# Attention's value product in two passes per head, with high and low values side by side in the stationary operand, and some weight sums moved behind attention

## The reference

```python
def _L0_xattn_ref(q, latent_kv, Wq, Wkv_expand, Wout):
    ...
    k, v = jnp.split(kv, 2, axis=-1)
    ...
    scores = jnp.einsum('bhqd,bhkd->bhqk', qh, kh) * inv_sqrt_d
    scores = jnp.where(causal, scores, jnp.finfo(scores.dtype).min)
    attn = jax.nn.softmax(scores, axis=-1)
    out = jnp.einsum('bhqk,bhkd->bhqd', attn, vh)
    return out.transpose(0, 2, 1, 3).reshape(b, sq, H) @ Wout.T

def weight_quant(w):
    scale = 1.0 / jnp.clip(jnp.mean(jnp.abs(w)), EPS_Q, None)
    return jnp.clip(jnp.round(w * scale), -1, 1) / scale

x = x + _L0_xattn_ref(_layernorm(x), ctx_512, Wq, Wkv_expand, Wout)
x = x + _L0_attn_ref(_layernorm(x), w_gate, norm_gate, w_down, norm_down)
x = x + _L0_ffn_ref(_layernorm(x), rms_weight, router_w, w_gate, w_up, w_down, sw_gate, sw_up, sw_down)
```

## Time and profile before

| | us |
|---|---|
| median of 3 runs | 635.94 (635.56 to 636.33) |
| span of the profiled execution | 633.0 |
| median less span | 2.9 |
| TensorE matmul busy in the span | 611.9 (97%) |
| VectorE busy | 524.0 (83%) |
| ScalarE busy | 421.6 (67%) |
| GpSimd busy | 148.1 (23%) |
| mean granted TensorE clock | 0.998 of full speed |

### The profile page before, as it was taken

How to read it: one execution, slowest core, us unless ns; L and a number is a source line. 1 busy time by engine, 2 the same in 40 slices (tenths; PEclk the granted TensorE clock), 3 DMA queues, 4 the chain that set the end, 5 groups by cost and what they waited for, 6 DMA issues and landing times.

```text
span 633.0 us, 10577 instructions
## 1 busy us (share of the span) xinstructions
PE 611.9 (97%) x3624; PEld 475.4 (75%) x3625; DVE 524.0 (83%) x886; ACT 421.6 (67%) x558; POOL 148.1 (23%) x167
## 2 busy tenths in 40 slices
PE   8899999998999999999989999999999999999996
PEld 6678888887886444444557888898988989889775
DVE  5888888878787777889999479789797988979686
ACT  4998888889755989784574366639376483855630
POOL 2354446416000333527920310000000000000051
PEclk9999999999999999999999999999999999999999
DMA  8977776765246997936999558796775968759257
GB/s 337 420 291 298 301 303 238 310 267 191 100 174 260 403 362 286 400 134 241 402 364 416 216 204 325 262 370 224 299 315 200 390 210 319 273 219 393 86 176 264
DMA packets 31070, 177.91 MB, mean 281 GB/s; under 512 B 4064, under 2 KB 4064, under 8 KB 14784
## 3 DMA queue, kind: packets, MB, share of 16 engines
q1 hardware_dynamic: 25536, 158.64, 65.3%
q0 software_dynamic: 5504, 18.88, 8.2%
HBM read 154.30 MB, written 23.20 MB: 280 GB/s over the span
## 4 chain that ended last, share of the span: by engine, by line
PE 50%; DVE 19%; ACT 14%; issue 8%; DMA 5%; POOL 2%; DVEq 1%; POOLq 0%; ACTq 0%; SPq 0%
PE BK L2132 10%; PE BK L306 9%; DVE WL L1029 4%; ACT RA L1383 4%; ACT PR L1410 4%; PE BK L2135 3%; PE BK L1882 3%; PE BK L312 3%; PE BK L318 3%; PE BK L313 3%; DMA RA<-wbit 2%; PE BK L2102 2%; PE BK L1827 2%; DMA RX<-wbit 1%; PE BK L2155 1%
## 5 line engine op out<-in xcount | busy, mean ns | idle before, releaser
L2132 PE MATMUL BK<-EX,WH 128*128 128x320 f32 x384 | 101.3, 344 | 0.3
L1029 DVE TENSOR_TENSOR WL<-RA,WH 128x2048 fp32r<-128x2048 f32 x40 | 89.4, 2287 | 7.6 <-ACT WH L1586 7.4
L2135 PE MATMUL BK<-EX,WL 128*128 128x160 f32 x336 | 79.3, 236 | 0.0
L1586 ACT ACTIVATE WH<-RA 128x2048 fp32r<-128x2048 f32 x40 | 73.6, 1910 | 0.2 <-PE BK L1925 0.2
L2132 PEld LDWEIGHTS BK<-EX,WH 128*128 128x128 f32 x384 | 69.7, 188 | 1.9 <-DVE SR L1069 1.9
L2135 PEld LDWEIGHTS BK<-EX,WL 128*128 128x128 f32 x336 | 64.1, 191 | 0.0
L705 POOL DMA_INDIRECT GA<-rows,SLOT x4 | 4.9, 1229 | 240.4 <-DVE WL L1029 239.5
L652 POOL TENSOR_TENSOR HB<-HB,ND (+2 forms) x26 | 28.6, 1121 | 100.5 <-DVE BH L915 99.9
L1482 ACT ACTIVATE RA<-RA,RT 128x2048 int16<-128x2048 f32 x22 | 43.7, 1998 | 3.8 <-DMA RA<-wbit 1.9
L1029 DVE TENSOR_TENSOR WL<-RC,WH 128x2048 fp32r<-128x2048 f32 x20 | 45.0, 2285 | 0.7 <-ACT WH L1586 0.7
L1882 PE MATMUL BK<-TG,XQ 128*128 128x512 bf16 x192 | 42.4, 379 | 0.1
(11 more groups left out here) (328 smaller groups left out, 1644.1 us busy)
## 6 DMA issues: line engine op xcount, KB each, us to landing
RA<-wbit SPq DMA_DIRECT2D x54, 1024.0 KB, 6.7
RA<-wmoe SPq DMA_DIRECT2D x40, 1024.0 KB, 6.5
RC<-wmoe SPq DMA_DIRECT2D x20, 1024.0 KB, 8.0
rows<-ZERO POOLq DMA_DIRECT2D x40, 256.0 KB, 8.2
XG<-rows SPq DMA_DIRECT2D x10, 512.0 KB, 3.7
rows<-YS SPq DMA_DIRECT2D x9, 512.0 KB, 6.0
RA<-wqk SPq DMA_DIRECT2D x7, 640.0 KB, 7.8
RA<-wo SPq DMA_DIRECT2D x4, 1024.0 KB, 7.5
```

The source lines that it names most:

```text
L1029: e.tensor_tensor(WL[m][:, q * RAW:q * RAW + RAW], RC[j][:, :], WH[m][:, q * RAW:q * RAW + RAW].bitcast(f32), ALU.subtract)\
L1586: e.activation(WH[m][:, q * RAW:q * RAW + RAW], RC[2 * m + q][:, :], ACT.Copy)\
L2132: mm = e.matmul(bank[GBK[f]][:, 0:2 * R], WH[m][:, at], EX[:, k, :, :].rearrange("p a b -> p (a b)"), start=k == 0, stop=k == KD - 1)
L2135: e.matmul(bank[GBK[f]][:, 0:R], WL[m][:, at], EX[:, k, 0, :], start=False, stop=False)
```

## The change

- **Value product.** VS holds, for each of four key blocks, high values of head 0, low values of head 0, low values of head 1, high values of head 1, 64 columns each; there are no zeros. A head's stationary operand is its high and low values side by side. Its moving operand is PTH, then PTL: two passes of four matmuls a head, 16 in place of 24 a pair. Low values x low probabilities are now included. Head 0 accumulates in bank 2, head 1 in bank 7. Since bank 2 is part of head 0's score strip, head 0 starts only when `probs_lo` has read the strip, and the third mask of the next scores waits until bank 2 is evacuated.
- **Evacuation.** VectorE copies the products with high values to AO (`values_out`), ScalarE those with low values to BT (`low_values`), 64 partitions each, per head. GpSimd adds them and splits the sum into OTH and OTL (`out_split`, three operations a pair, one or two steps later). The last pair is added and split by VectorE and ScalarE.
- **Weight sums.** Four of the down chunks (29 to 32) are no longer summed in attention. RA[4] is not loaded in the steps any more, which now all have three sums. In ScalarE's step the sum of RA[3] comes right behind the exponentials and that of RA[1] before the query split; VectorE's sum of RA[2] comes before `probs_lo`. SP's order is RA[0], 1, 2, 3 as before. The four chunks are loaded into XQ's and RD's space and summed by ScalarE under the output projection (`late_load`, `late_absum`); the scale of the down weights is made later, by a matmul and `down_scales`.
- **Order.** In ScalarE's last step `wo_hi(0)` comes before the query split and `wo_hi(1)` behind `values_hi`. `k_split` of VectorE comes between the two halves of `probs_lo`. `down_load(1)` is issued later.

```diff
-        VH = a("VH", [P, NT, 3, HD], f32r)
-        VL = a("VL", [P, NT, 3, HD], f32r)
+        VS = a("VS", [P, NT, 4, HD], f32r)
+        BT = a("BT", [P, TOK], f32)
...
             for j in (1, 2, 3):
-                sum_load(j, 11 + j, 1)
-            sum_load(4, 10, 1)
+                sum_load(j, 9 + j, 1)
             e.dma_start(WR[:, :, :], wrt).then_inc(s("norm_in"), 16)
 
             def pair_loads(c):
                 qk_load(c)
                 for j in (1, 2, 3):
-                    sum_load(j, c * 3 + 8 + j, c)
-            for c in (2, 3, 4):
-                pair_loads(c)
-                sum_load(4, (11, 31, 32)[c - 2], c)
-            with e.Fori(5, NPAIR - 1) as c:
+                    sum_load(j, c * 3 + 6 + j, c)
+            with e.Fori(2, NPAIR - 1) as c:
                 pair_loads(c)
             qk_load(NPAIR - 1)
-            e.wait_ge(free_a[4], 5)
+            e.wait_ge(free_a[4], 1)
             wo_load(0)
-            sum_load(1, 30, NPAIR - 1)
+            sum_load(1, 28, NPAIR - 1)
             e.wait_ge(free_a[3], NPAIR - 1)
...
-            e.wait_ge(s("ot_lo"), NPAIR + 1)
+            e.wait_ge(s("av_pe"), 2 * NPAIR)
             e.dma_start(NG[:, :], n_gate.partition_broadcast(P)).then_inc(s("norm_in"), 16)
+
+            def late_load(j, chunk):
+                e.dma_start(DS[j][:, :], wbit[chunk]).then_inc(s(("raw_8", "raw_d")[j]), 16)
+            e.wait_ge(s("t_pe"), 2 * NPAIR)
+            late_load(0, 29)
 
             def bit_load(j, chunk, name, uses):
                 e.wait_ge(s(name), uses)
@@ -479,8 +486,13 @@
             def down_load(i, name):
                 e.dma_start(down_raw(i)[:, :], wbit[2 * GC + i]).then_inc(s(name) if isinstance(name, str) else name, 16)
             e.wait_ge(s("wo_d"), 2)
+            late_load(1, 30)
             for n in range(4):
                 bit_load(n, 4 + n, "tern", 1 + n)
+                if n in (1, 3):
+                    e.wait_ge(sum_x[0], 3 + n // 2)
+                    late_load(1, 31 + n // 2)
+            e.wait_ge(sum_x[0], 5)
             down_load(1, "raw_d")
...
+            def out_split(c):
+                at = bass.ds(c, 1)
+                e.wait_ge(s("av_ev1"), c * 2 + 4)
+                e.tensor_tensor(AO[:, :], AO[:, :], BT[:, :], ALU.add).then_inc(s("ot_hi"), 1)
+                e.wait_ge(s("ot_hi"), c * 2 + 1)
+                hi = OTH[:, at, :].rearrange("p a n -> p (a n)")
+                e.tensor_tensor(hi.rearrange("p (a b) -> p a b", b=P), AO[:, :].rearrange("p (a b) -> p a b", b=P),
+                                ONEF[:, :].rearrange("p (a b) -> p a b", a=1).to_broadcast([P, TOK // P, P]), ALU.mult)\
+                    .then_inc(s("ot_hi"), 1)
+                e.wait_ge(s("ot_hi"), c * 2 + 2)
+                e.tensor_tensor(OTL[:, at, :].rearrange("p a n -> p (a n)"), AO[:, :], hi.bitcast(f32), ALU.subtract)\
+                    .then_inc(s("ot_lo"), 1)
...
-            def probs_lo(c):
+            def probs_lo(c, between=None):
                 for h in range(2):
+                    if h and between is not None:
+                        k_split(between)
                     e.wait_ge(s("pt_hi"), c * 2 + h + 1)
                     e.tensor_tensor(PTL[h][:, :], STR[h][:, 0:STRIP], PTH[h][:, :].bitcast(f32), ALU.subtract)\
                         .then_inc(s("pt_lo"), 1)
 
-            def out_lo(c):
-                at = bass.ds(c, 1)
-                e.wait_ge(s("ot_hi"), c + 1)
-                e.tensor_tensor(OTL[:, at, :].rearrange("p a n -> p (a n)"), bank[7],
-                                OTH[:, at, :].rearrange("p a n -> p (a n)").bitcast(f32), ALU.subtract)\
-                    .then_inc(s("ot_lo"), 1)
+            def values_out(c, to=AO):
+                e.wait_ge(s("ot_lo"), c + 1 if to is AO else NPAIR - 1)
+                for h in range(2):
+                    e.wait_ge(s("av_pe"), c * 2 + h + 1)
+                    e.tensor_copy(to[HEADS[h], :], bank[VALUE_BANKS[h]][HEADS[h], :]).then_inc(s(("av_ev0", "av_ev1")[h]), 1)
...
             def pair(c, more):
                 row_maxima(c - 1)
                 normalise(c - 1)
-                k_split(c)
-                probs_lo(c - 1)
+                if more:
+                    absum(2, bass.ds(c * 3 + 8, 1), c * 16 + 16)
+                probs_lo(c - 1, c)
                 q_split(c)
-                if more:
-                    absum(2, bass.ds(c * 3 + 10, 1), c * 16 + 16)
-                else:
+                values_out(c - 1)
+                if not more:
                     wo_lo(0)
-                out_lo(c - 1)
...
+            values_out(NPAIR - 1, AO_LAST)
             wo_lo(2)
-            out_lo(NPAIR - 1)
+            e.wait_ge(s("av_ev0"), 2 * NPAIR)
+            e.wait_ge(s("av_ev1"), 2 * NPAIR + 2)
+            e.tensor_tensor(AO_LAST[:, :], AO_LAST[:, :], BO_LAST[:, :], ALU.add).then_inc(s("av_ev0"), 1)
+            e.wait_ge(s("av_ev0"), 2 * NPAIR + 1)
+            e.wait_ge(s("av_ev1"), 2 * NPAIR + 3)
+            e.tensor_tensor(OTL[:, NPAIR - 1, :], AO_LAST[:, :], OTH[:, NPAIR - 1, :].bitcast(f32), ALU.subtract)\
+                .then_inc(s("av_ev0"), 1)
             absum(1, slice(0, 1), 16 * (NPAIR + 1))
...
+            e.wait_ge(sum_x[0], 5)
+            e.tensor_reduce(WS[:, 1:2], ACCW[:, 2 * GC:NABS], AX.X, ALU.add).then_inc(s("wsum"), 1)
             gate_rows(3)
             gate_scale(slice(3, 4))
+            down_scales()
             for n, (c, t) in enumerate(HEAD):
...
-            def out_hi(c):
-                e.wait_ge(s("av_pe"), c + 1)
-                e.activation(OTH[:, bass.ds(c, 1), :].rearrange("p a n -> p (a n)"), bank[7], ACT.Copy)\
-                    .then_inc(s("ot_hi"), 1)
+            def low_values(c, to=BT):
+                e.wait_ge(s("ot_lo"), c + 1 if to is BT else NPAIR - 1)
+                for h in range(2):
+                    e.wait_ge(s("av_pe"), c * 2 + h + 1)
+                    e.activation(to[HEADS[h], :], bank[VALUE_BANKS[h]][HEADS[1 - h], :], ACT.Copy)\
+                        .then_inc(s(("av_ev0", "av_ev1")[h]), 1)
...
             def pair(c, more):
                 exponentials(c - 1)
+                if more:
+                    absum(3, bass.ds(c * 3 + 9, 1), c * 16 + 16)
+                else:
+                    absum(1, slice(28, 29), 16 * NPAIR)
                 k_split(c)
                 probs_hi(c - 1)
                 if more:
-                    absum(1, bass.ds(c * 3 + 9, 1), c * 16 + 16)
-                else:
-                    absum(1, slice(30, 31), 16 * NPAIR)
-                q_split(c)
-                if more:
-                    if isinstance(c, int):
-                        absum(4, slice(*((10, 11), (11, 12), (31, 32), (32, 33))[c - 1]), c * 16 + 16)
-                    absum(3, bass.ds(c * 3 + 11, 1), c * 16 + 16)
+                    absum(1, bass.ds(c * 3 + 7, 1), c * 16 + 16)
                 else:
                     wo_hi(0)
+                q_split(c)
+                low_values(c - 1)
+                values_hi(c)
+                if not more:
                     wo_hi(1)
-                out_hi(c - 1)
-                values_hi(c)
-            for c in (1, 2, 3, 4):
-                pair(c, True)
-            with e.Fori(5, NPAIR - 1) as c:
+            with e.Fori(1, NPAIR - 1) as c:
                 pair(c, True)
             pair(NPAIR - 1, False)
             exponentials(NPAIR - 1)
@@ -1465,10 +1503,18 @@
             probs_hi(NPAIR - 1)
             e.wait_ge(s("vp_lo"), NPAIR)
             wo_hi(2)
-            absum_kept(4, 3, 16 * 7, None)
-            absum_kept(3, 2, 16 * (NPAIR + 1), (free_a[4], 6))
-            out_hi(NPAIR - 1)
+            low_values(NPAIR - 1, BO_LAST)
+            absum_kept(4, 3, 16 * 3, None)
+            absum_kept(3, 2, 16 * (NPAIR + 1), (free_a[4], 2))
+            e.wait_ge(s("av_ev0"), 2 * NPAIR + 1)
+            e.activation(OTH[:, NPAIR - 1, :], AO_LAST[:, :], ACT.Copy).then_inc(s("av_ev1"), 1)
             absum_kept(2, 1, 16 * (NPAIR + 1), (free_a[3], NPAIR))
+
+            def late_absum(n):
+                e.wait_ge(s("raw_d" if n else "raw_8"), 16 * max(n, 1))
+                e.activation(DS[n > 0][:, :], DS[n > 0][:, :], ACT.Abs, accum_out=ACCW[:, 29 + n:30 + n])\
+                    .then_inc(sum_x[0], 1)
+            late_absum(0)
...
             def attend(c, more):
 
-                if more:
-                    e.wait_ge(s("k_lo"), c + 2)
                 e.wait_ge(s("vp_lo"), c + 1)
-                for n, (V1, P1, h) in enumerate(((VH, PTH, 0), (VL, PTH, 0), (VH, PTH, 1), (VL, PTH, 1),
-                                                 (VH, PTL, 0), (VH, PTL, 1))):
-                    if n in (0, 2):
-                        e.wait_ge(s("pt_hi"), c * 2 + h + 1)
-                    elif n > 3:
-                        e.wait_ge(s("pt_lo"), c * 2 + h + 1)
-                    for j in range(NT):
```

(35 more changed lines are left out.)

39 lines of the change are left out of this document (23 added, 16 removed).

## The result

| | before | after |
|---|---|---|
| median of the timed runs, us | 635.8 (635.56 to 636.33) | 651.89 (647.25 to 654.25) |
| ratio, 95% interval | | 1.0242 (1.0212 to 1.0271) |
| span of the profiled execution, us | 633.0 | 645.5 |
| mean granted TensorE clock there | 0.998 | 0.990 |
| TensorE begins pair 7, T(7) | 130.79 | 134.43 (forecast 134.2) |

The prediction took T(8) for the start of the output projection, which before is also the end of the scores. After, the two lie 0.53 us apart: TensorE waits there for VectorE's `wo_lo(0)`, which now stands behind the copies of the products. From here on T(8) is the end of the scores.

A forecast was written before the change was run, and what follows sets the result against it. Attention looked bound by TensorE before, and after the change by a loop of loads and weight sums. 3.4 - 0.9 + 3.5 = 6.0 us: span 639.0 against 633.0, timed 641.9 us, range 637.5 to 644.5.

The forecast's parts named there:

- TensorE's part: Value product in each attention step: 16 matmuls for 24, 2.53 us for 3.80, so 1.27 us less a step.
- The evacuation: Product copies out of PSUM: 64-partition copies cost as much as full ones, 0.59 us on ScalarE, 0.69 on VectorE.
- The loop: Attention steps: SP's load issue, third chunk's landing and ScalarE's sums take 16.67 us a step; T(7) 3.4 us later.
- The last step: Last attention step, without such a load: 14.7 us against 15.57 before, 0.9 us gained.
- The tail: From T(8) to the second output tile: 23.15 us against 19.7 before, 3.5 us lost, bounds 2.5 and 4.
- Work moved behind attention: Under the output projection: four late weight sums, their loads and the later scale cost 0 us, bound 1.
- The third rival: More delay than seen, such as GpSimd's longer work delaying VectorE's divisions in each step: over 644.5 us; chance 0.05.
- The first rival: Attention steps: chunks land early enough, TensorE stays the bound, steps of 14.4 to 14.8 us, 631.5 us; chance 0.13.

The follow-up runs named there:

- e2: The changed kernel with SP issuing each step's three chunks in the order RA[3], RA[2], RA[1]; 643.51 us.
- e6: The kernel before with only ScalarE's sum of RA[3] moved behind the exponentials and VectorE's sum of RA[2] behind the divisions; 637.86 us.
- e5: e3 with one more wait: GpSimd's out_split waits in each step until that step's divisions are done; 635.36 us.
- e3: The changed kernel with both GpSimd's wait before v_lo(7) put back and the load order RA[3], RA[2], RA[1]; 637.54 us.
- e1: The changed kernel with GpSimd's dropped wait on pn put back before v_lo(7); 645.93 us.
- e4: The kernel before with only GpSimd's wait on pn before v_lo(7) dropped; 641.34 us.
- e7: The changed kernel with useless matmuls (24, 20 and 14) ahead of TensorE's three long waits of the last pair; 650.62 us.
- e8: e7 with 8 more useless matmuls at the start of each step; 650.26 us.

## Why the prediction was wrong, step by step

- **TensorE's part: right.** The value product is 2.5 us a pair (2.53 forecast) wherever the clock is full.
- **The evacuation at full price: right.** The copies of 64 partitions take 0.69 on VectorE and 0.59 on ScalarE, as the full ones did.
- **The loop, +3.4 at T(7): right, +3.6.** 16.6 to 16.8 us a step where 16.67 was worked out; T(7) 134.43 for 134.2. TensorE waits about 1 us before the value product, ScalarE up to 1.8 for the third chunk. e2 took the loop away by changing the order of the loads alone, and e6 made it without the new value product: shown both ways. The third chunk landed 9.7 us after the first issue (96.89 to 106.58, the end of the chain's 8.63), with 9.75 worked out from the rows. The Trainium skill's page DMA: Bandwidth & Descriptors, section Anatomy of one DMA, has a fit for GpSimd's path, and the estimate by it was 9.2 us for the three chunks and a loop of 16.1. These loads are on SP's queue, and the trace shows them slower than that.
- **The last step, 0.9 gained: nearly.** To the end of the scores, 14.96 against 15.57 is 0.6. The mask did not wait, but the transposes took 2.67 us for 2.11 before (2.11 in e5, where the divisions are shielded). T(8) is 3.0 later, with 2.5 forecast. To the first matmul of the output projection, as the prediction had T(8), it is 3.6 later and next to nothing is gained; the 0.53 us lie in front of a wait for `wo_lo(1)` that would have been longer by as much.
- **The tail, +3.5: this is the step that failed. It measured +9.7.** The cause is a line that the working left out: the removed wait of GpSimd on `pn`. Its effect stands in the prediction's own row, the 2.67 us before `v_lo`, and the mechanism in the row beside it, 3.62 against 2.29 us for a VectorE operation beside GpSimd; they were applied to `wo_lo(2)` and not to the divisions. With the wait put back and the loop gone (e3) the tail is 23.2 us, which is the 23.15 of the sum. Up to the end of the value product the steps of that sum hold too (T(8) + 13.45 in both); behind it some luck is in the match, since `wo_lo(2)` was done at T(8) + 16.9 instead of 17.5 and TensorE waited for VectorE's last weight sum instead. By medians the wait is worth 6.0 us (e1) in the changed kernel and 5.5 in the one before (e4); e4 shows it alone.
- **The clock: no term in the sum.** TensorE's longer idle times let the clock fall to half, which stretched the last value product from 2.5 to 4.0 us. Of the tail's excess of 6.2 us over the forecast, e7 takes away 1.0 by keeping the clock up; the other 5.2 are the divisions'.
- **Work moved behind attention, at nothing: right.** From the second output tile to the end it is 466.8 us, 467.0 before. ScalarE waited 2.07 for one late chunk (until 200.19) and VectorE some 2 us for its sum, under TensorE's matmuls.
- **The third rival** named GpSimd's longer work and VectorE's divisions, but in each step, at 0.05. In the steps it is there: 2.31 instead of 1.27 us, but the loop of SP and ScalarE bounds the step and doesn't pass through them. Once the loop is gone it is worth 0.64 us a step (15.53 to 14.89, e5). Where it decided was the tail.
- **The first rival** (steps of 14.4 to 14.8) needed the other load order as well as the shielded divisions: e5's 14.9 is nearly that.

By medians the account is: of 16.1 us, taking the loop away gives back 8.4 (more than the 3.6 that it cost, since the steps then fall under those of before: T(8) is 5.8 earlier than after, and the rest is in the open point below), the wait 6.0, and keeping `out_split` off the divisions in the steps 2.2 (e3 to e5). That ends 0.4 us under before. What the change can gain stands in e5: T(8) is 6.1 us earlier than before (140.3 against 146.4), the tail takes 4.3 of that back (24.0 against 19.7), and behind the tail another 1.1 goes.

Open stays why the changed kernel's other runs are 4 to 7 us longer than its profiled one. Their mean clock is lower (0.981 to 0.983, against 0.990), but where it fell no profile shows. The timed runs spread over 7.0 us; either edit alone makes it little (e1 2.5 us, with the loop left; e2 2.2 us, with the divisions' delay left), and fillers do so less (e7 5.1, e8 3.9). The late chunk in e7's profile shows one way in which such a run can lose 3 us: in the loop a late landing delays all that follows. That the longer runs of the changed kernel had one is not shown.

## What to carry to other kernels

Read a diff for the waits that it removes as well as for those it adds: a wait that costs its own engine 2.7 us may be what keeps that engine out of another's way. When VectorE works from SBUF to SBUF on the critical path, look at which GpSimd instruction is under way: in these runs VectorE's divisions waited for that one's end. Short ones cost less than a long one (2.31 us for a group of four against 7.54), and a semaphore in the right place less still (1.27). With one buffer per load and one queue in program order, issue first the load whose buffer comes free first; else the step can become the sum of the landings and sums behind it, as here (16.7 us against 15.5).
